# Fourteen weight tiles and twelve result tiles for the expert blocks, addresses read earlier, rows issued three blocks ahead of weights

## The reference, cut to what matters

```python
h = tok(x)                                  # convs, norms, feed-forward, max-pool: 375 -> 373 positions
h = h + attn(layernorm(h))                  # softmax(q k^T) x
xf = layernorm(h)
w  = softmax(relu(xf @ gw1 + gb1) @ gw2 + gb2)
top_w, top_idx = top_k(w, 2); top_w = softmax(top_w)
for e in range(8):                          # combine[:, e] is top_w where e was chosen, else 0
    out += combine[:, e:e+1] * (gelu(xf @ we1[e] + be1[e]) @ we2[e] + be2[e])
out = h + out
```

## Time and profile before

| | us |
|---|---|
| median of 3 runs (222.42 to 529.38) | 222.91 |
| the profiled execution, its own time | 221.66 |
| its span, first to last instruction | 219.9 |
| PE busy (L1189 and L1182 are dense expert work) | 204.4 |
| DVE busy | 154.4 |
| ACT busy | 136.9 |
| POOL busy | 112.9 |
| bytes moved by DMA, 35.31 MB, mean | 161 GB/s |
| mean granted TensorE clock | 0.993 of full speed |

### The profile page before, as it was taken

The page is one execution under the profiler, slowest core; times in us unless marked ns, Lnnn a source line. Parts: engine busy times, 40 slices in busy tenths (PEclk is TensorE's granted clock), DMA queues, the critical chain, the costliest instruction groups (busy, mean ns, idle before and its releaser), DMA issues.

```text
span 219.9 us, 5429 instructions
## 1 busy us (share of the span) xinstructions
PE 204.4 (93%) x1553; PEld 166.6 (76%) x1553; DVE 154.4 (70%) x688; ACT 136.9 (62%) x302; POOL 112.9 (51%) x168
## 2 busy tenths in 40 slices
PE   6997788999999999999999999999999989699990
PEld 5864656659857986898678967889989768599780
DVE  6379999998998998979599944484426233224895
ACT  2234997998989688776679248456655547335430
POOL 7746776611630147676774775015777766472000
PEclk9999999999999999999999999999999999999997
DMA  5999999940010012102111121587597898712773
GB/s 157 244 270 305 330 405 406 402 170 3 0 35 1 3 35 58 53 23 80 52 47 37 38 70 48 141 259 246 165 308 232 286 303 304 270 36 71 195 226 106
DMA packets 26000, 35.31 MB, mean 161 GB/s; under 512 B 4083, under 2 KB 18838, under 8 KB 25971
## 3 DMA queue, kind: packets, MB, share of 16 engines
q1 hardware_dynamic: 23137, 30.60, 43.4%
q0 software_dynamic: 2240, 4.00, 5.8%
q10 hardware_dynamic: 594, 0.36, 0.6%
HBM read 10.61 MB, written 14.39 MB: 114 GB/s over the span
## 4 chain that ended last, share of the span: by engine, by line
PE 71%; DVE 8%; SPq 6%; ACT 5%; issue 4%; DMA 3%; POOL 1%; DVEq 0%; ACTq 0%
PE PS L1189 11%; PE PS L1182 10%; PE PS L1124 7%; PE PS L1106 7%; PE PS L1214 5%; PE PS L1205 4%; PE PS L989 4%; PE PS L1113 4%; DMA blk_x<-xs 3%; PE PS L1001 3%; SPq L444 3%; PE PS L1101 3%; PE PS L1018 2%; SPq L436 2%; DVE acc L965 2%
## 5 line engine op out<-in xcount | busy, mean ns | idle before, releaser
L547 POOL DMA_INDIRECT ys<-yblk,blk_x x37 | 36.0, 973 | 28.1 <-DVE yblk L956 19.3
L517 POOL TENSOR_TENSOR rstd<-mv,mhalf 125x3 f32<-125x3 f32 x32 | 27.7, 867 | 41.0 <-DVE mv L698 40.7
L661 ACT ACTIVATE gd<-PS,bias 128x373 f32<-128x373 f32 x48 | 27.1, 574 | 15.4 <-PE PS L1182 10.8
L541 POOL DMA_INDIRECT xs<-rows_x,pos_x x30 | 29.9, 996 | 13.0 <-issue 8.4
L1182 PE MATMUL PS<-xt_sb,w_all 128*128 128x373 f32 x96 | 35.7, 482 | 0.0
L1189 PEld LDWEIGHTS PS<-w_all,gd 128*125 128x125 f32 x288 | 33.6, 187 | 2.1
L1189 PE MATMUL PS<-w_all,gd 128*125 128x128 f32 x288 | 34.6, 273 | 0.0
L672 ACT ACTIVATE gb_t<-PS,blk_w 128x128 f32<-128x128 f32 x58 | 18.1, 365 | 15.1 <-issue 8.8
L930 DVE SCALAR_TENSOR_TENSOR x_sb<-PS,comb,x_sb 125x128 f32<-125x128 f32 x72 | 20.7, 343 | 5.8 <-PE PS L1189 4.9
L1182 PEld LDWEIGHTS PS<-xt_sb,w_all 128*128 128x128 f32 x96 | 15.7, 190 | 5.0 <-issue 0.9
L956 DVE TENSOR_TENSOR yblk<-PS,blk_w 128x128 f32<-128x128 f32 x29 | 8.4, 290 | 15.8 <-PE PS L1214 15.5
(11 more groups left out here) (201 smaller groups left out, 409.4 us busy)
## 6 DMA issues: line engine op xcount, KB each, us to landing
blk_w<-w_all SPq DMA_DIRECT2D x29, 321.0 KB, 3.1
xs<-blank SPq DMA_DIRECT2D x1, 8256.0 KB, 25.3
blk_x<-xs SPq DMA_DIRECT2D x37, 64.5 KB, 3.0
yg<-ys SPq DMA_DIRECT2D x5, 336.0 KB
x_sb<-in_x SPq DMA_DIRECT2D x4, 336.0 KB
out<-x_sb SPq DMA_DIRECT2D x8, 168.0 KB
xt_sb<-in_xt SPq DMA_DIRECT2D x3, 375.0 KB, 5.4
w_all<-in_we SPq DMA_DIRECT2D x1, 1024.0 KB
```

The costliest lines, as they stand in the source:

```text
L517: pool.tensor_tensor(rstd[i][:, n % 2, :], mv[i][:, n % 2, :, 1], mhalf[:], ALU.pow)\
L541: pool.indirect_dma_start(xs, bass.IndirectOffsetOnAxis(ap=pos_x[:, b // 2, s, i:i + 1], axis=0), rows_x[:, k, s, j, :], None, bounds_chec ...
L547: pool.indirect_dma_start(ys, bass.IndirectOffsetOnAxis(ap=blk_x[n % SLOTS][:, t, D:XW].bitcast(u32), axis=0), yblk[n % YBUF][:, t, :], No ...
L661: act.activation(gd[:, k % GD, c, 0:TP], of("D1", n)[:, 0:TP], ACT.Gelu, bias=bias128[:, 2 + k % E * HC + c:3 + k % E * HC + c]).then_inc( ...
```

## The change

There are 14 weight tiles in place of 7. The first seven are tiles of their own, as before; the other seven share one new array, `late`, with `prob` and `prob_t`. `lw.15`, the first to use one of these, waits until the last `at` is done. `lw.n` now waits for `yv.(n-14)`. There are 12 `yblk` tiles in place of 6. Eight of the 18 row tiles are now slices of `blank`. The weight tiles' semaphores are ones that were used for the input loads, with their earlier count added to the value that is waited for. In SP's order all 29 addresses are read before block 8's rows: 13 of them before `od.0` (8 before), eleven between `od.0` and `lx.0` (eleven before), and the last five between `lx.7` and `lx.8`. Rows 8 to 11 are issued before `lw.8`, and from there `lx.(n+4)` stands between `lw.n` and `lw.(n+1)`. No other engine's order is changed.

```diff
-WSLOTS = 7
-YBUF = 6
+WSLOTS = 14
+OWN = 7
+YBUF = 12
...
 SP_ORDER = """
-c4.1 c4.2 c4.3 c4.4 c4.5 rg.8 rg.9 rg.10 rg.11 rg.12 rg.13 rg.14 rg.15 od.0 rg.16 rg.17 rg.18 rg.19 rg.20 rg.21
-rg.22 rg.23 rg.24 rg.25 rg.26 lx.0 lx.1 lx.2 lx.3 lx.4 lx.5 lx.6 lx.7 lx.8 lw.8 lx.9 lw.9 lx.10 lw.10 lx.11 lw.11
-rg.27 lx.12 rg.28 lw.12 lx.13 lw.13 lx.14 lw.14 lx.15 rg.29 rg.30 lw.15 lx.16 lw.16 lx.17 lw.17 lx.18 lw.18 lx.19
-lw.19 rg.31 lx.20 lw.20 rg.32 rg.33 lx.21 lw.21 lx.22 lw.22 lx.23 lw.23 lx.24 lw.24 rg.34 lx.25 lw.25 lx.26 lw.26
-lx.27 lw.27 lx.28 lw.28 rg.35 lx.29 lw.29 lx.30 lw.30 lx.31 lw.31 lx.32 lw.32 lx.33 lw.33 lx.34 lw.34 rg.36 lx.35
-lw.35 lx.36 lw.36 yl.0 yl.1 yl.2 od.1 yl.3 out.0 yl.4 out.1 out.2 out.3 od.2 out.4
+c4.1 c4.2 c4.3 c4.4 c4.5 rg.8 rg.9 rg.10 rg.11 rg.12 rg.13 rg.14 rg.15 rg.16 rg.17 rg.18 rg.19 rg.20 od.0 rg.21
+rg.22 rg.23 rg.24 rg.25 rg.26 rg.27 rg.28 rg.29 rg.30 rg.31 lx.0 lx.1 lx.2 lx.3 lx.4 lx.5 lx.6 lx.7 rg.32 rg.33
+rg.34 rg.35 rg.36 lx.8 lx.9 lx.10 lx.11 lw.8 lx.12 lw.9 lx.13 lw.10 lx.14 lw.11 lx.15 lw.12 lx.16 lw.13 lx.17
+lw.14 lx.18 lw.15 lx.19 lw.16 lx.20 lw.17 lx.21 lw.18 lx.22 lw.19 lx.23 lw.20 lx.24 lw.21 lx.25 lw.22 lx.26
+lw.23 lx.27 lw.24 lx.28 lw.25 lx.29 lw.26 lx.30 lw.27 lx.31 lw.28 lx.32 lw.29 lx.33 lw.30 lx.34 lw.31 lx.35
+lw.32 lx.36 lw.33 lw.34 lw.35 lw.36 yl.0 yl.1 yl.2 od.1 yl.3 out.0 yl.4 out.1 out.2 out.3 od.2 out.4
...
-        prob = sb("prob", [P, 2, NJ, TP])
+        late = sb("late", [128, (WSLOTS - OWN) * WROW])
+        prob = late[0:P, 0:2 * NJ * TP].rearrange("p (s j t) -> p s j t", s=2, j=NJ)
-        prob_t = sb("prob_t", [P, 2, NJ, TE])
+        prob_t = late[0:P, 2 * NJ * TP:2 * NJ * (TP + TE)].rearrange("p (s j t) -> p s j t", s=2, j=NJ)
...
-        blk_x = [sb(f"blk_x{i}", [128, NT, XW]) for i in range(SLOTS)]
-        blk_w = [sb(f"blk_w{i}", [128, WROW]) for i in range(WSLOTS)]
+        blank = sb("blank", [128, RI, XW])
+        blk_x = [sb(f"blk_x{i}", [128, NT, XW])[:] for i in range(SLOTS - RI)] + [blank[:, r:r + 1, :] for r in range(RI)]
+        blk_w = [sb(f"blk_w{i}", [128, WROW])[:] for i in range(OWN)]\
+            + [late[:, i * WROW:(i + 1) * WROW] for i in range(WSLOTS - OWN)]
...
-        s_bw = [sem(f"s_bw{i}") for i in range(WSLOTS)]
+        s_bw = ([(s, 32) for s in s_x] + [(s_xt[0], 32)] + [(s, 16) for s in s_xt[1:]] + [
+            (S[v], 16 * m) for v, m in (("wc", 1), ("we", 2), ("b64", 2), ("wm", 2), ("rows6", 1), ("wmid", 3))])[:WSLOTS]
...
                 if name == "lw":
                     k = n - E
                     if k == 0:
                         sp.wait_ge(S["be1"], 1)
+                    if k == OWN:
+                        wait(sp, "at", B)
                     if k >= WSLOTS:
                         wait(sp, "yv", n + 1 - WSLOTS)
```

More of the change, by code:

```diff
@@ L287, in audio_tower @@
         tiny = sb("tiny", [1, 1])
-        blank = sb("blank", [128, RI, XW])
         gd = sb("gd", [128, GD, HC, TE])
@@ L363, in weights @@
                 return w_all[:, n, :]
-            eng.wait_ge(s_bw[(n - E) % WSLOTS], 16 * ((n - E) // WSLOTS + 1))
-            return blk_w[(n - E) % WSLOTS][:]
+            s, first = s_bw[(n - E) % WSLOTS]
+            eng.wait_ge(s, first + 16 * ((n - E) // WSLOTS + 1))
+            return blk_w[(n - E) % WSLOTS]
         def xn4_of(n):
@@ L435, in _ @@
                     wait_so(sp, n - SLOTS)
-                    sp.dma_start(blk_x[i][:], xs[bass.ds(row_of_block[n], BLK), :].rearrange("(p t) d -> p t d", t=NT))\
+                    sp.dma_start(blk_x[i], xs[bass.ds(row_of_block[n], BLK), :].rearrange("(p t) d -> p t d", t=NT))\
                         .then_inc(s_bx[n % LOADS], 16)
@@ L441, in _ @@
                         sp.wait_ge(S["be1"], 1)
+                    if k == OWN:
+                        wait(sp, "at", B)
                     if k >= WSLOTS:
                         wait(sp, "yv", n + 1 - WSLOTS)
-                    sp.dma_start(blk_w[k % WSLOTS][:], w_all[:, bass.ds(row_of_block[n] // CAP, 1), :].rearrange("p o d -> p (o d)"))\
-                        .then_inc(s_bw[k % WSLOTS], 16)
+                    sp.dma_start(blk_w[k % WSLOTS], w_all[:, bass.ds(row_of_block[n] // CAP, 1), :].rearrange("p o d -> p (o d)"))\
+                        .then_inc(s_bw[k % WSLOTS][0], 16)
                 if name == "yl":
```

## The result

The changed kernel takes 219.24 us in the median of six runs, against 222.4 for the kernel before on the same chip, so 3.2 us less. The forecast was 218.6, in a range of 217.7 to 220.6. The profiled execution took 219.27 us, its span 217.5 (221.66 and 219.9 before).

What follows compares the result with a forecast made beforehand. PE's work was taken to bound the kernel nearly everywhere, except where late rows from SP's queue stalled it: 4.37 us of stalls less 0.1 left for other waits saves 4.3, so 222.9 becomes 218.6 us, range 217.7 to 220.6.

Steps and rivals of the forecast that it cites:

- What bounds it: Whole kernel: PE's work bounds nearly everywhere; from 170 to 190 us it waits for rows that SP's queue issues late.
- All four stalls go: minus 4.37: PE's waits for rows at T.24, T.27, T.28 and T.33, with small rests, vanish, saving 4.37 us.
- the allowance of 0.1: Block stage: 0.1 us (0 to 0.5) left for PE's transposes waiting for ACT and DVE, now hidden by the stalls.
- The forecast's own range: Main case, rows no longer late: saves 3.8 to 4.8 us, 218.1 to 219.1 us in total, chance 0.70.
- Addresses ahead of od.0 and lx.8: SP: five reads ahead of each, 3.2 us, covered by 3.5 us at od.0 and 4.1 us at T.8; cost nothing.
- lw.n at 145.9 + 1.32 (n - 8): SP's weight loads: lw.8 issued at 145.9 us, each later one 1.32 us on, lw.36 at 182.9.
- the 1.4 that was named as a sign of being wrong: SP's row and weight pairs: taking over 1.4 us each would show the forecast wrong.
- The turn at 1.63 us a pair: SP's issuing from lw.8 to lw.36: at 1.63 us a pair the gain is gone; it shrinks from 1.48.
- The 0.5 us that POOL falls back fits: Tail: POOL's scatters gain 3.8 us where PE gains 4.3; the load between yl.0 and fin.0 absorbs the difference.
- the rival that was given 0.18: Weights become the late ones, or POOL holds the tail: saves 2.2 to 3.8 us, about 219.9; chance 0.18.
- The slower pace: Rival: SP's pairs from lw.8 to lw.36 slow down; at 1.75 us each the time is 226.2; chance 0.05.
- 29 pairs at 1.37 us: Argument against the rival that DMA engines bound (222.9, chance 0.07): from 143.6 us the pairs end at 185.6, not 190.

Runs made afterwards that it cites:

- e4: Kernel before with all addresses read before block 8's rows, pairs and tiles as before; takes 3.3 us off the 55.42 us up to yv.36.
- e6: Changed kernel with 13 extra address reads, one ahead of every second row load from lx.12 on; 79.34 us from T.0 to the end.
- e10: Changed kernel with row and weight loads in the old pair order, tiles and early addresses kept; 51.14 us up to yv.36, 75.53 from T.0 to the end.
- e11: Changed kernel with 5 in place of 12 warm-up matmuls in the second group; median 217.94 us, ratio 0.9779.
- after: The changed kernel in its first profile, against the kernel before; median 219.24 us, ratio 0.9861, 74.6 us from T.0 to the end.
- e1: The changed kernel profiled again with nothing altered; span 216.0 us, block stage 51.62 us.
- e3: Kernel before with SP's whole new order but 7 weight and 6 result tiles; 51.25 us up to yv.36, 76.13 from T.0 to the end.
- e8: Changed kernel with five more warm-up matmuls, on a tile of their own, ahead of everything PE does; ratio 0.9874.
- e7: Changed kernel with 25 extra address reads, one ahead of every row load from lx.12 on; 84.95 us from T.0 to the end.
- e9: Kernel before with 38 in place of 6 warm-up matmuls ahead of the first piece; 78.72 us from T.0 to the end, against 78.48.

## Why the prediction was right, and where it was off

**What bounds it.** Right: SP's sequence, not the DMA engines. e4 takes 3.3 us with the reads alone, e6 loses 4.7 by thirteen reads, and the DMA share stayed at 0.88 (the earlier trace rows has the same) while PE was busy. The Trainium skill ("DMA: Bandwidth & Descriptors", "Issuing engines are not separate DMA queues") calls the time to issue a DMA usually small beside the DMA itself. For a single one that agrees: 0.4 to 0.5 us of issue, and 3.1 us in the median until a weight load has landed. Summed over 29 pairs and ten address reads on one queue it was what made the rows late here.

**"All four stalls go: minus 4.37", with 0.1 left.** The stalls went. With every wait gone (e10, e11) the stage saves 4.28 and 4.27, so 4.37 was 0.1 high. The term that was mis-sized is the allowance of 0.1, and its cause was another than forecast: not waits of PE's transposes for ACT and DVE, but weights that landed late, 0.33 us ahead of L1.31 in after and 0.40 ahead of L1.33 in e1. So the stage saved 3.86 and 3.80. In e3, e8, e10 and e11 it saved 4.0 to 4.3. The forecast's own range, 3.8 to 4.8, held them all, at its edge.

**Addresses ahead of od.0 and lx.8.** Right. od.0's wait fell from 3.5 to 0.2 us, that at lx.0 rose from 0.6 to 1.1. lx.8 went out at 144.91, by the later T.0 143.45, against 143.6 forecast.

**"lw.n at 145.9 + 1.32 (n - 8)".** lw.8 at 147.12 is 145.7 by that T.0, right. The pace of the pairs was 1.47, above the 1.4 that was named as a sign of being wrong, and lw.33 went out 40.95 us behind T.0 in place of 37.5. Two issues of 1.79 and 1.75 us, each at a code fetch (packets of 2111 and 1979 ns at 156.6 and 173.3), hold 2.7 us more than usual, 0.11 a pair; without them it is 1.36. The rows could stand it: none was issued less than 6.9 us ahead of its transpose. The weights could not quite. The prediction took 3.1 us for every landing and looked for the tight place at blocks 12 to 14 and at lw.36; it was at lw.31 in after and at lw.33 in e1. From lw.33 on SP has no rows left and issues weight loads 0.7 us apart, and of these the two whose landing e1 records, lw.33 and lw.35, took 5.41 and 5.82 us; a code fetch at 184.2 lies in both.

**The turn at 1.63 us a pair.** Near in number, at another place. It was worked out for lw.36 with 28 equal steps. In e6 the longest waits stand ahead of L1.23 (1.4 us) and L1.31 (1.9 us), and none at L1.36. At 1.61, counted as the prediction does, e6 was 0.9 us slower than before, so an estimate of the turn is 1.61 - 0.9 / 28 = 1.58; counted by real pairs up to lw.31 it is 1.71 - 0.9 / 23 = 1.67.

**POOL and the tail.** so.36 was to start 3.8 us sooner: from T.0 it came 53.13 us in place of 57.01, 3.9. "The 0.5 us that POOL falls back fits" held in the profile of after, and is thinner than I wrote: a fetch inside that landing costs 1.3 to 1.8 us, and did in three of the seven profiles with the faster stage (after, e1, e3, e4, e8, e10, e11). I had carried over one number, the 1.2 us from the last scatter to yl.0, though the earlier trace rows already showed that one kind of transfer can take 2.69 or 4.95 us.

**The sum.** 4.3 us forecast, 3.2 measured in the medians (3.0 for e1), 3.9 between two profiles that start alike. 0.4 of the rest is the allowance. The other 0.7 is not shown by any single run; it fits the start (T.0 differs by 1.6 us between two profiles of the same kernel) and a tail of 24.4 to 24.9 in place of 23.1 us in some runs, but that is argued. By the medians the saving lies outside the forecast's 3.8 to 4.8 and inside the 2.2 to 3.8 of the rival that was given 0.18, weights or POOL taking part of it. That rival did happen, in part: the weights took 0.4 us in both profiles of the changed kernel, and the landing of the last scatter 1.3 us or more in three others. So the mechanism was right and the total held with the help of the wide range. The slower pace came too, at 1.47, and was covered; e6 and e7 show where it is not.

**Two slips in the working.** 29 pairs at 1.37 us end at 185.6 counted from lw.8 at 145.9; from 143.6, as written, it is 183.3. An address at 0.6 us a load would cost 0.64 - 0.26 + 0.6 = 0.98 us, not 0.95. Neither changes the forecast.

## What to carry to other kernels

A queue that issues every transfer of a loop is a resource with a time per iteration: add it up beside the engines', and take out of the loop what can be done ahead of it (here ten address reads, 3.3 of the 3.9 us). Order and buffer depth on top of that are worth trying one at a time: here the tiles bought nothing that the order did not. Whatever is moved to the back of the queue is what runs late next, and a small wait left over may be its first sign. Where a stall ends behind one slow transfer, ask what was on the DMA engines in that microsecond before pricing all transfers by the median.

## What the runs showed of the hardware

**Code fetches slow the transfers around them.** About every 240 of PE's 3106 matmul and weight load instructions (13 in the run, 14 with 240 or 128 more; 140 to 290 between two) queue 8 moves 16384 bytes in one packet, 0.9 to 2.4 us on one DMA engine. That this is PE's code is inferred from these counts. What is in flight then tends to land late: in the profiles of before, after and e1 to e11, the recorded landings from block 9 on are 1.8 to 3.8 us for the 44 row loads without a packet in them (median 2.6) and 2.6 to 5.4 for the 14 with one (median 4.2); for weight loads 2.5 to 4.1 (74, median 3.1) and 2.6 to 5.8 (32, median 4.2). A long landing also has more room for a packet, so these medians alone don't prove the cause. A last scatter frees its reader 2.8 to 3.3 us later in place of 1.2. That a load is spread over all 16 engines and waits for the one that is taken is argued, not shown; that the longest stall moves with the fetch is shown by e9, in one profile.

**The clock at the start varies.** With the same work the full grant came between 4.89 and 8.18 us, worth about 1.5 us at T.0. In e4, e7, e10 and e11 the granted clock also fell to half for 3.4 us from 19.7 to 20.0 us on, and in e7 and e9 it fell for as long inside the block stage (at 194.12 and 186.86 us; in e9 PE had been idle for 2.1 us when it fell). The stretches up to 40 us of e10 (with the fall), and then of e1 (without):

```profile
0.00:20.00 20.00, 16.64 (x177) 12.19 (x177) 12.54 (x44) 5.33 (x10) 13.01 (x42) 1.00 0.93 236
20.00:40.00 20.00, 17.57 (x183) 12.31 (x183) 17.60 (x87) 16.15 (x29) 12.72 (x21) 0.92 1.07 373
```

```profile
0.00:20.00 20.00, 16.65 (x191) 12.73 (x194) 13.18 (x47) 6.00 (x11) 12.99 (x42) 1.00 0.91 229
20.00:40.00 20.00, 17.02 (x181) 12.05 (x172) 19.00 (x95) 17.54 (x33) 14.26 (x24) 1.00 1.08 371
```

PE was busy for 16.64 and 16.65 us ahead of it, so its busy time over those 20 us does not tell the two apart. Two profiles with and without the fall can't be compared by their spans, only from a point behind it.
